# Residuals stored early, one DMA a pair, and a batch norm added onto them by accumulating DMAs

## The reference, cut to what matters

```python
def _L0_conv_ref(x, g, b, w_qkv, w_out, b_out):     # x: (8, 64, 32, 32) f32
    xn = (x - mean) / jnp.sqrt(var + EPS) * g + b    # over the 64 channels
    ...                                              # linear attention, 8 heads of 32
    out = jnp.einsum('bchw,oc->bohw', out, w_out) + b_out[None, :, None, None]
    return out + xn                                  # x of the next stage: the residual

def _L1_conv_ref(x, W, gamma, beta):
    y = conv3x3(jnp.sign(x), jnp.sign(W))            # padding 1
    mean, var = jnp.mean(y, axis=(0, 2, 3)), jnp.var(y, axis=(0, 2, 3))
    inv = gamma / jnp.sqrt(var + BN_EPS)
    yn = (y - mean[None, :, None, None]) * inv[None, :, None, None] + beta[None, :, None, None]
    return yn + x
```

## Time and profile before

| | before |
|---|---|
| time, median of 3 runs | 99.69 us (99.69 to 99.94) |
| span of the profiled execution | 98.3 us |
| PE busy | 81.6 us (83%) |
| DVE busy | 62.3 us (63%) |
| ACT busy | 56.7 us (58%) |
| POOL busy | 41.6 us (42%) |
| written to device memory | 2.10 MB |
| read from device memory | 2.51 MB |

### The profile page before, as it was taken

The page is one execution under the profiler, slowest core; times in us unless marked ns, Lnnn a source line. Parts: engine busy times, 40 slices in busy tenths (PEclk is TensorE's granted clock), DMA queues, the critical chain, the costliest instruction groups (busy, mean ns, idle before and its releaser), DMA issues.

```text
span 98.3 us, 2063 instructions
## 1 busy us (share of the span) xinstructions
PE 81.6 (83%) x771; PEld 47.5 (48%) x771; DVE 62.3 (63%) x119; ACT 56.7 (58%) x110; POOL 41.6 (42%) x55
## 2 busy tenths in 40 slices
PE   4999988999999999999999999999999999100000
PEld 4923423368575457565756656767564545100000
DVE  4826787967399509546885599539717297669600
ACT  2225957788898477087691745868313296189000
POOL 6999281283295442071693391859100000006400
PEclk9999999999999999999999999999999999995555
DMA  1998013104200213000042000714400808105893
GB/s 46 306 352 311 7 53 105 53 9 122 86 3 0 68 51 100 1 0 0 0 136 81 0 0 0 168 52 83 130 7 0 198 22 183 30 0 148 257 322 127
DMA packets 4748, 8.89 MB, mean 90 GB/s; under 512 B 1430, under 2 KB 1746, under 8 KB 4740
## 3 DMA queue, kind: packets, MB, share of 16 engines
q1 hardware_dynamic: 3540, 7.46, 26.0%
q0 software_dynamic: 336, 1.05, 3.4%
q10 hardware_dynamic: 864, 0.26, 1.1%
HBM read 2.51 MB, written 2.10 MB: 47 GB/s over the span
## 4 chain that ended last, share of the span: by engine, by line
PE 70%; DVE 11%; ACT 7%; issue 4%; ACTq 1%; POOLq 1%; POOL 1%; DVEq 0%
PE ps L832 8%; PE ps L846 8%; PE ps L833 7%; PE ps L734 5%; PE ps L922 5%; PE ps L933 4%; PE ps L858 4%; PE ps L903 4%; PE ps L797 4%; DVE mx L573 4%; PE ps L973 3%; PE ps L878 3%; PE ps L885 3%; PE ps L864 2%; DVE XN L548 2%
## 5 line engine op out<-in xcount | busy, mean ns | idle before, releaser
L578 DVE TENSOR_REDUCE mxp<-ps 128x2 bf16<-128x1024 f32 x12 | 14.7, 1224 | 11.3 <-PE ps L797 11.3
L423 ACT ACTIVATE E<-ps 128x512 f32<-128x512 f32 x32 | 17.8, 596 | 3.3 <-PE ps L833 3.2
L330 POOL TENSOR_TENSOR E_lo<-E 128x512 bf16<-128x512 f32 x11 | 12.5, 1162 | 7.2 <-ACT E L423 7.1
L832 PE MATMUL ps<-wk_max,S 128*128 128x256 bf16 x64 | 15.2, 275 | 0.0
L833 PE MATMUL ps<-wk_lo,S 128*128 128x256 bf16 x64 | 15.1, 272 | 0.0
L335 POOL DMA_DIRECT2D out<-OUT x3 | 1.8, 606 | 20.2 <-DVE OUT L724 20.2
L298 POOL TENSOR_TENSOR x_lo<-XN,x_hi 128x512 bf16<-128x512 f32 x8 | 9.2, 1155 | 2.5 <-DVE x_hi L554 2.4
L352 ACT ACTIVATE sq<-ps 128x512 f32<-128x512 f32 x8 | 4.8, 603 | 8.2 <-PE ps L734 8.2
L734 PE MATMUL ps<-X,center_mat 128*128 128x512 f32 x16 | 9.4, 693 | 0.0
L287 POOL CAST x_hi<-XN 128x512 bf16<-128x512 f32 x6 | 3.7, 612 | 13.4 <-DVE XN L548 13.4
L644 DVE SCALAR_TENSOR_TENSOR X<-XN,vec,ps 128x1024 f32<-128x1024 f32 (+1 forms) x5 | 5.2, 1066 | 5.4 <-PE ps L903 5.4
(11 more groups left out here) (137 smaller groups left out, 158.9 us busy)
## 6 DMA issues: line engine op xcount, KB each, us to landing
X<-in_x SPq DMA_DIRECT2D x3, 512.0 KB, 5.0
X<-X SPq DMA_DIRECT2D x4, 256.0 KB, 3.6
X<-X SPq DMA_DIRECT2D x8, 128.0 KB, 2.3
S<-x_hi SPq DMA_DIRECT2D x7, 126.0 KB
S<-x_lo SPq DMA_DIRECT2D x7, 126.0 KB
out<-OUT SPq DMA_DIRECT2D x3, 256.0 KB, 4.0
out<-OUT POOLq DMA_DIRECT2D x3, 256.0 KB, 4.5
X<-in_x SPq DMA_DIRECT2D x2, 256.0 KB, 3.7
```

Source lines behind the costliest of these rows:

```text
L330: nc.gpsimd.tensor_tensor(e_lo, e, e_hi, ALU.subtract).then_inc(elo_pool, 1)
L423: nc.scalar.activation(E[:, b % 2, 2 * g:2 * g + 2, :].rearrange("p k j -> p (k j)"), kt_ps[g % 2], ACT.Exp).then_inc(exp_ready, 1)
L578: nc.vector.tensor_reduce(mxp[:, h, :, t], k_ps, AX.X, ALU.max).then_inc(max_ready, 1)
L832: nc.tensor.matmul(dst, chunk, wk_max[:, b % 2, :], start=True, stop=False)
```

## The change

The tile `X1` and its twelve moves are gone. As soon as `add_input` of a pair is done, the sync engine stores that pair of `X` to the output by one plain DMA of 512 KB. At the end ScalarE and VectorE share the parts: ScalarE does (4), (6,7) and (0), and VectorE does (5), (2,3) and (1). Each does scale and shift in one instruction out of `ps` (or `Y`). GpSimd then issues two DMAs for each of the six parts, twelve in all, which add `OUT` to what is in the output. Before it issues them it waits for the part and for the plain stores of the residuals there. The sync engine issues nothing at the end and waits for all stores.

```diff
-    SCALED = ((4,), (5,), (6, 7), (1,), (0,), (2, 3))
-    ADDED = ((4,), (5,), (6, 7), (0, 1), (2, 3))
+    ACT_FINALS = ((4,), (6, 7), (0,))
+    DVE_FINALS = ((5,), (2, 3), (1,))
+    FINALS = ((4,), (5,), (6, 7), (2, 3), (0,), (1,))
...
-    out_d = out.rearrange("b c h w -> b c (h w)")
+    out_banks = out.rearrange("(k d) c h w -> k d c (h w)", d=2)
+    out_pairs = out.rearrange("(q d) c h w -> q (d c) (h w)", d=2)
...
-            for q in two:
+            for q in range(PAIRS):
                 sp.wait_ge(x1_ready, HALVES * (q + 1))
-                for d in two:
-                    sp.dma_start(X1[q * C:(q + 1) * C, 2 * d:2 * d + 2, :], X[d * C:(d + 1) * C, q, :]
-                                 ).then_inc(x1_moved[q], 16)
-            for q in range(2, PAIRS):
-                sp.wait_ge(x1_ready, HALVES * (q + 1))
-                for d in two:
-                    for h in range(HALVES):
-                        sp.dma_start(X1[h * C:(h + 1) * C, 2 * q + d, :],
-                                     X[d * C:(d + 1) * C, q, h * BANK:(h + 1) * BANK]).then_inc(x1_moved[q], 16)
...
-            sp.wait_ge(stored, 16 * 5)
-            sp.wait_ge(stored_pool, 16 * 5)
+                sp.dma_start(out_pairs[q], X[:, q, :]).then_inc(x1_stored[q], 16)
+            for q in range(PAIRS):
+                sp.wait_ge(x1_stored[q], 16)
+            sp.wait_ge(stored, 16 * 2 * len(FINALS))
...
+            for part in FINALS:
+                wait_finished(pool, part)
+                for q in ((0, 1) if part[0] < 4 else (part[0] // 2,)):
+                    pool.wait_ge(x1_stored[q], 16)
+                for k in two:
+                    if part[0] < 4:
+                        dst = out_banks[k, part[0] // 2][:, (part[0] % 2) * BANK:(part[-1] % 2 + 1) * BANK]
+                    else:
+                        dst = out_h[k, :, part[0]:part[-1] + 1, :]
+                    src = OUT[k * C:(k + 1) * C, part[0]:part[-1] + 1, :]
+                    pool.dma_start(dst, src if part[0] >= 4 else src.rearrange("c b n -> c (b n)"),
+                                   accum_op=ALU.add).then_inc(stored, 16)
...
-            act.wait_ge(scale_ready, 1)
-            for part in SCALED:
+            act.wait_ge(affine_ready, 1)
+            for part in ACT_FINALS:
                 nc.scalar.activation(images(OUT, part), images(ps, part) if part[0] else Y[:], ACT.Identity,
-                                     scale=bn[:, BN_SCALE]).then_inc(t_ready, 1)
+                                     bias=bn[:, BN_SHIFT], scale=bn[:, BN_SCALE]).then_inc(done_act, 1)
...
-            for part in ADDED:
-                dve.wait_ge(t_ready, max(SCALED.index(p) + 1 for p in SCALED if set(p) <= set(part)))
-                for q in ((0, 1) if part[0] < 4 else (part[0] // 2,)):
-                    dve.wait_ge(x1_moved[q], 16 * (2 if part[0] < 4 else 4))
-                nc.vector.scalar_tensor_tensor(images(OUT, part), images(OUT, part), bn[:, BN_SHIFT],
-                                               images(X1, part), op0=ALU.add, op1=ALU.add).then_inc(o_ready, 1)
+            for part in DVE_FINALS:
+                nc.vector.tensor_scalar(images(OUT, part), images(ps, part), bn[:, BN_SCALE], bn[:, BN_SHIFT],
+                                        ALU.mult, ALU.add).then_inc(done_dve, 1)
```

More of the change, by code:

```diff
@@ L115, in attention_then_binary_conv @@
         SG = sb("SG", [P, PAIRS, H + 2, W + 2], bf16)
-        X1 = sb("X1", [P, B, BANK])
         OUT = sb("OUT", [P, B, BANK])
@@ L181, in attention_then_binary_conv @@
         f_done, x1_ready, sg_ready = sem("f_done"), sem("x1_ready"), sem("sg_ready")
-        x1_moved = [sem(f"x1_moved{q}") for q in range(PAIRS)]
+        x1_stored = [sem(f"x1_stored{q}") for q in range(PAIRS)]
         conv_done, y_ready, st_ready, st_act = sem("conv_done"), sem("y_ready"), sem("st_ready"), sem("st_act")
@@ L186, in attention_then_binary_conv @@
             sem("mv_ready"), sem("fold_done"), sem("bn_act"), sem("scale_ready"), sem("affine_ready"))
-        t_ready, o_ready, stored, stored_pool = sem("t_ready"), sem("o_ready"), sem("stored"), sem("stored_pool")
+        done_act, done_dve, stored = sem("done_act"), sem("done_dve"), sem("stored")
         def wait_hi(engine, n):
@@ L193, in wait_hi, with wait_finished @@
                 engine.wait_ge(hi_ready, n - 1)
-        def wait_added(engine, part):
-            engine.wait_ge(o_ready, ADDED.index(part) + 1)
+        def wait_finished(engine, part):
+            if part in ACT_FINALS:
+                engine.wait_ge(done_act, ACT_FINALS.index(part) + 1)
+            else:
+                engine.wait_ge(done_dve, DVE_FINALS.index(part) + 1)
         act_records = ST[:, ACT_STATS[0]:ACT_STATS[-1] + 1, :].rearrange("p b (r e) -> p (b r) e", e=3)
```

## The result

The changed kernel takes 106.49 us (median of 4 runs, 105.98 to 106.78) against 99.81 us for the kernel before in the same session (4 runs, 99.69 to 100.16). The ratio is 1.067, with a 95% interval of 1.063 to 1.071: slower by 6.7 us. The forecast was 104.5 us in a range of 99.4 to 108.5. The profiled execution of the changed kernel took 106.32 us, with a span of 104.5.

What follows compares the result with a forecast made beforehand. The prediction took the output's drain through the DMA engines as the bound: start at 89.1, plus 12.8 us for 4.19 MB at 328 GB/s, plus 0.6, 0.6 and 1.4, gives 104.5 us. The range was 99.4 to 108.5.

Steps and rivals of the forecast that it cites:

- main term: Final drain: adding DMAs also fetch 2.10 MB, so 4.19 MB come in at 328 GB/s, 12.8 us for 8.0.
- Part 1: Residuals: four early 512 KB stores replace twelve SBUF moves, worth nothing; last lands by 84.1 to 86.9, margin 3 us.
- Part 2: Scale and shift on ScalarE and VectorE: 2.55 and 2.6 us, done at 89.4; last part ready 3.1 us sooner.
- rival (c): GpSimd's issuing: an adding DMA costs double, 1.15 us; last start 100.4, low DMA share, time 105.6; chance 0.08.
- Rival (b): Final drain: fetch and write of a piece follow one another, pace nearer 215 GB/s; 107.9 to 111.2 us; chance 0.15.
- the sum: Whole tail: start 89.1, transfers 12.8, then 0.6, 0.6 and 1.4 outside the span, giving 104.5 us.
- Part 3: GpSimd's issuing of twelve final DMAs: 0.57 to 0.86 us each; at 0.57, 6.9 us, last start 94.1.
- rival (a): Final drain: fetch hidden, GpSimd's issuing bounds the end; 99.3 us, with variants 98.7 and 101.2; chance 0.28.

Runs made afterwards that it cites:

- two-queue run: Changed kernel with plain instead of adding final stores, lower 64 partitions from the sync engine's queue, upper 64 from GpSimd's; residual missing from output: 99.12 us, ratio 0.9924.
- run with the first part sooner: Kernel before, with bank 4's part finished by one VectorE instruction once the scale is there, so its stores start sooner: 99.66 us, ratio 0.9992.
- plain traffic: Changed kernel with plain final stores, plus twelve sync-engine loads from the input into an unused tile, shaped and timed like the adding DMAs' fetches: 105.58 us, ratio 1.055.
- run with a quarter to move: Changed kernel with each of the twelve adding DMAs cut to 16 of its 64 rows, a quarter of pieces and bytes: 101.75 us, one run.

## Why the prediction was right, and where it was off

**Right, step by step.** The end before was not set by VectorE's supply: the two-queue run has all parts ready 3 us sooner and gains 0.5 us. That the drain alone set it is less firm, as the run with the first part sooner shows. The forecast's main term, the fetch of 2.10 MB through the same engines, was a bound from rows. Leaving the adding out brings the time down to 100.20 us, and plain traffic that fetches and stores the same pieces brings it back to 105.58, at the same pace and with the engines full; so the term is shown, except that this traffic also writes what it fetches.

By the Trainium skill, Collectives: The Full Stack ("Why ReduceScatter is half of AllGather"), an add takes two source reads and so runs at half the rate of a copy. The trace agrees: the engines spend 13.5 us on the adding DMAs and 7.1 on the plain ones, 1.9 times as much, though by the estimate above about 1.1 us of the difference go with the smaller packets.

The starts stood 0.57 us apart, as counted from the earlier trace rows. Part 1 held: nothing waited for the early stores. Part 2 held nearly: all parts were ready 2.8 us after the shift's end for 2.6, and that they were ready at 89.2 for 89.4 is because the shift ended 0.4 us sooner.

**Where it was lucky.** The prediction took one pace for the whole drain, 328 GB/s of incoming bytes. Twice the bytes written is 252 GB/s in the first five microseconds and 350 behind, so neither stretch ran at it; the mean, 4.19 MB in 13.6 us, is 308. The size of the term came out near by this balance, and why the first stretch is slow isn't known.

**The signs that it named.** The share of 0.95 to 1.05 and 156 GB/s written from 89 to 102 (for 165) were there. The last wait ended at 103.8, just inside the 104 behind which the prediction was to count as wrong. GpSimd's instructions showed over 1 us each, which had been named as the sign of rival (c), a doubled issue. Yet (c) isn't what happened: it asked for starts 1.15 us apart and a low share, the starts stood 0.57 apart at a full share, and with eight larger DMAs, GpSimd done 3 us sooner, the time fell by one. Rival (b), fetch and write one after another, asked for 107.9 us and more.

**Terms that were mis-sized.** The profiled execution took 106.3 where the sum gave 104.5, 1.8 us more. The transfers took about 13.6 us and not 12.8 (+0.8, and 0.1 back from their start at 89.0 for 89.1). From the last bytes at about 102.6 to the end of the wait at 103.8 were 1.2 us and not 0.6 (+0.6; with the trickle until 103.3 counted as transfer, this 0.6 belongs to the line before); from there to the span's end 0.7 and not 0.6 (+0.1). Outside the span lie 1.8 us and not 1.4 (+0.4). The 1.4 was the median less the span of a single execution whose own time was not known; over 29 runs of the kernel before the part outside the span was 2.1, so by that figure the execution of the profile took some 0.7 us more than the median.

**Part 3 was half right.** The prediction took the issue as one number, the distance from start to start. For adding DMAs the two differ: a start every 0.57 us, but 0.88 us to make one (10.57 over twelve), so the work piles up behind the starts. The value lay just above the 0.57 to 0.86 taken, and it was said to be hidden, which it is for the whole output. The sum there, though, let the last DMA land 3.2 to 4.8 us after its start; it took 9.9. The run with a quarter to move shows the floor that this makes: 101.75 us, well above rival (a)'s 99.3 for "issuing bounds the end". **Rival (a)**, and with it any chance of faster, thus had a better excluder than its pace: even with a free fetch, twelve adding DMAs would not be made in time, by that one run. Its own sum, for plain DMAs, was good: 99.3 with ends of 98.7 and 101.2, against the 100.20 of the plain stores.

**Part 1's price for the store** was too high: it took loads of the same size, 3.9 to 6.7 us. The four stores landed so:

```profile
L251 SPq DMA_DIRECT2D out<-X x4: 332/340/358, 60.5 to 79.8; - x4
...
DMA to landing us min/median/max: 2.6/2.6/2.8
```

The margin was larger than stated, and the outcome the same.

**Still open.** The plain traffic leaves 1.2 points of the ratio (1.055 to 1.067) to the adding itself, or to one queue where the imitation had two, and it writes 2.10 MB more than the adding does, so its 5.1 points are not the fetch alone; the intervals are 1.049 to 1.060 and 1.063 to 1.071. And the drain is slow in its first five microseconds, 126 against 175 GB/s, without the rows telling why. And the run with the first part sooner gained less than the reading of the drain gave.

## What to carry to other kernels

Where the end of a kernel is the drain of its output, a DMA that adds moves work from an engine with slack to the one resource that has none: count the bytes that it fetches too, and not only those that it writes. Before speeding up the instructions ahead of the stores, ask what the drain would take if all were ready at once; here a supply 3 us sooner was worth 0.5. For the making on a queue, take the time from the first start to the last end, not the distance between starts: here 10.57 us for twelve, where the starts alone gave 6.9.

## What the runs showed of the hardware

- An adding DMA from GpSimd costs 0.8 to 0.9 us to make, nearly whatever it moves (twelve: 9.68 us for 224 pieces, 10.57 for 896; eight of 256 KB: 7.50 us); a plain one of the same shape 0.53 to 0.55.
- For 2.10 MB of adding DMAs the 16 engines were busy for 13.5 us, for the same bytes as plain stores 7.1. With half the bytes, 896 pieces took 9.72 us and 448 took 8.45.
- Adding DMAs put one row in a packet (1088 packets, with 2 KB rows mostly), GpSimd's plain ones 4 KB (704 packets), for the same 2.10 MB. The sync engine's plain stores in the two-queue run put one row in a packet as well (544 packets for 1.05 MB, GpSimd's 352), and took no more of the engines for it: 3.2 us against 3.7.
- Stores of 512 KB with 4 KB rows landed in 2.6 us; the same 2.10 MB as moves inside SBUF kept the engines busier, a share of 0.38 against 0.23 over the stretch from 60 to 84 us, at 89 GB/s in both. The kernel before:

```profile
60.00:84.00 24.00, 23.52 (x327) 13.85 (x326) 15.21 (x29) 13.66 (x27) 6.01 (x6) 1.00 0.38 89
```

The changed kernel:

```profile
60.00:84.00 24.00, 23.11 (x325) 13.45 (x323) 15.22 (x29) 13.26 (x26) 6.01 (x6) 1.00 0.23 89
```
